# Latent attention over the context: the ends and beginnings of batches in other steps, and the residual norm in halves

## The reference, cut to the stage that is touched

```python
# layer 2, cross attention: x is the context (4, 77, 128), latents the stream (4, 512, 128), H = 8 heads of DH = 64
xn = _ln(x, g_x, b_x)
ln = _ln(latents, g_l, b_l)
q = ln @ w_q
kv_in = jnp.concatenate([xn, ln], axis=1)
k, v = jnp.split(kv_in @ w_kv, 2, axis=-1)
q, k, v = (split(q) * scale, split(k), split(v))
sim = jnp.einsum('bhid,bhjd->bhij', q, k)
sim = jnp.where(m, sim, -jnp.finfo(sim.dtype).max)
attn = jax.nn.softmax(sim, axis=-1)
out = jnp.einsum('bhij,bhjd->bhid', attn, v)
return _ln(out @ w_out, g_o, b_o)
# and around it, in the decoder
x = _layernorm(x + _L2_xattn_ref(ctx_1024, x, ...), axis=-1)
```

## Times and profile before

| | us |
|---|---|
| median of three executions | 2083.51 |
| lowest, highest | 2081.59, 2091.36 |
| the profiled execution | 2109.39 |
| its span | 2107.5 |
| the stage's loop in it, 1069.96 to about 1398 | some 328 |

### The profile page before, as it was taken

The page is one execution under the profiler, slowest core; times in us unless marked ns, Lnnn a source line. Parts: engine busy times, 40 slices in busy tenths (PEclk is TensorE's granted clock), DMA queues, the critical chain, the costliest instruction groups (busy, mean ns, idle before and its releaser), DMA issues. The chain is left out here.

```text
span 2107.5 us, 33370 instructions
## 1 busy us (share of the span) xinstructions
PE 1716.1 (81%) x11732; PEld 1022.0 (48%) x11822; DVE 1422.6 (68%) x3275; ACT 1075.5 (51%) x2294; POOL 416.6 (20%) x576
## 2 busy tenths in 40 slices
PE   4779858999977999985789999973699988796773
PEld 3546533333365666663644444432345444464662
DVE  4546578888764776765666767767699999575224
ACT  3346526777723445444455565543477777463221
POOL 0110030000032666652200000001200000100654
PEclk8999889999978999997999999995699999997896
DMA  4000000000025888861000000000000000001454
GB/s 121 1 1 2 1 1 0 1 1 1 1 94 199 315 327 324 334 238 42 1 1 0 1 1 1 1 1 18 1 1 2 2 1 1 1 2 51 136 156 129
DMA packets 42862, 132.29 MB, mean 63 GB/s; under 512 B 7106, under 2 KB 22635, under 8 KB 37611
## 3 DMA queue, kind: packets, MB, share of 16 engines
q1 hardware_dynamic: 32523, 116.98, 15.9%
q0 software_dynamic: 4992, 10.23, 1.5%
q10 hardware_dynamic: 5184, 2.95, 0.5%
HBM read 120.27 MB, written 14.58 MB: 64 GB/s over the span
## 5 line engine op out<-in xcount | busy, mean ns | idle before, releaser
L160 POOL TENSOR_SCALAR rstd<-MV 128x2 f32<-128x2 f32 (+1 forms) x100 | 27.0, 270 | 1014.6 <-DVE MV L128 1008.9
L855 DVE TENSOR_REDUCE l1aM<-PS 128x2 f32<-128x1024 f32 x128 | 152.9, 1220 | 22.6 <-PE PS L611 20.5
L773 ACT ACTIVATE l1aE<-PS 128x512 f32<-128x512 f32 x256 | 140.8, 595 | 48.7 <-PE PS L640 45.4
L773 ACT ACTIVATE l3aE<-PS 128x512 f32<-128x512 f32 (+3 forms) x256 | 102.5, 442 | 47.6 <-PE PS L644 44.8
L855 DVE TENSOR_REDUCE l3aM<-PS 128x2 f32<-128x256 f32 (+3 forms) x128 | 101.3, 819 | 20.7 <-PE PS L613 19.6
L2748 ACT COPY PT<-PS 128x512 f32<-128x512 f32 x128 | 68.9, 590 | 87.7 <-PE PS L2659 87.4
L2838 DVE TENSOR_REDUCE M<-PS 128x1 f32<-128x589 f32 x128 | 92.4, 764 | 24.0 <-PE PS L2648 23.7
L1879 PE MATMUL PS<-WB,H 128*128 128x512 f32 x234 | 107.7, 597 | 0.0
L2754 ACT ACTIVATE E<-PS,M 128x589 f32<-128x589 f32 x128 | 95.9, 763 | 19.4 <-DVE M L2838 19.3
L883 DVE SCALAR_TENSOR_TENSOR l3aE<-l3aE,l3aLB 128x2048 f32<-128x2048 f32 (+1 forms) x64 | 94.9, 1483 | 2.7 <-ACT l3aE L773 2.7
L611 PE MATMUL PS<-l1aKS,l1aQS 128*128 128x512 bf16 x249 | 76.8, 388 | 16.2 <-DVE l1aQS L878 5.5
(11 more groups left out here) (686 smaller groups left out, 4488.2 us busy)
## 6 DMA issues: line engine op xcount, KB each, us to landing
WB<-in_experts SPq DMA_DIRECT2D x39, 1286.0 KB
TB<-mixed_tails SPq DMA_DIRECT2D x39, 768.5 KB
WB<-in_experts SPq DMA_DIRECT2D x39, 384.0 KB
mixed_tails<-in_tails SPq DMA_DIRECT2D x1, 2305.5 KB, 12.2
cols_fold_sb<-in_cols_fold SPq DMA_DIRECT2D x1, 1676.0 KB, 12.1
mixed_tails<-in_tails SPq DMA_DIRECT2D x1, 1537.0 KB, 16.1
mixed_tails<-WB SPq DMA_DIRECT2D x2, 768.5 KB, 4.2
cols_l2x_sb<-in_cols_l2x SPq DMA_DIRECT2D x1, 1154.0 KB, 9.1
```

Source lines behind the costliest of these rows:

```text
L773: nc.scalar.activation(E[0:kn, home(m, kt) + j, q0:S], PS[0:kn, 4 + n % 2, q0:S], ACT.Exp, scale=SCALE).then_inc(exp_done, 1)
L855: v.tensor_reduce(M[:, m % 2, qt, 2 * hp:2 * hp + 2], PS[:, bank:bank + 2, 0:kc], AX, ALU.max, negate=True).then_inc(pair_free, 1)
```

## The change

The table of endings gets eight entries instead of six: I and Y are split into halves of two of the four row tiles each (I0, I1, Y0, Y1). The steps within the batch become these:

| unit | before | after |
|---|---|---|
| L, M, T, U | 6, 7, 8, 9, late | 0, 2, 3, 4, late |
| W, X, G, H | 5, 6, 7, 8 | 5, 6, 7, 8 |
| I | 9 | 10 and 12 (halves) |
| Y | 10 | 14 and 15 (halves) |
| the 14 projection units, two to a step | 9 to 15 | 8 to 14 |

```diff
+    ENDING = ("W", "X", "G", "H", "I0", "I1", "Y0", "Y1")
...
-            for i, c in enumerate("WXGHIY"):
-                late.setdefault(s0 + 5 + i, []).append((c, b - 1))
+            for c, at in zip(ENDING, (5, 6, 7, 8, 10, 12, 14, 15)):
+                late.setdefault(s0 + at, []).append((c, b - 1))
...
-            for i, u in enumerate(todo[:4]):
-                late.setdefault(s0 + 6 + i, []).append(u)
+            for u, at in zip(todo[:4], (0, 2, 3, 4)):
+                late.setdefault(s0 + at, []).append(u)
             for i, u in enumerate(todo[4:]):
-                (late, early)[i % 2].setdefault(s0 + 9 + i // 2, []).append(u)
+                (late, early)[i % 2].setdefault(s0 + 8 + i // 2, []).append(u)
...
-                elif kind == "I":
+                elif kind == "I1":
                     k.norm_gpsimd(pool, b, b)
...
-                elif kind == "I":
+                elif kind in ("I0", "I1"):
                     dve.wait_ge(y_done, 3 * b + 3)
-                    k.norm_stats(dve, Y[:, :, :], step, b)
-                elif kind == "Y":
-                    k.norm_apply(dve, normed, b, b)
+                    half = int(kind[1])
+                    k.norm_half_stats(Y[:, HALVES[half]], step, b, HALVES[half])
+                elif kind in ("Y0", "Y1"):
+                    k.norm_half_apply(dve, normed, b, b, int(kind[1]))
```

More of the change, by code:

```diff
@@ L2518, in latent_attention @@
         if b:
-            for i, c in enumerate("WXGHIY"):
-                late.setdefault(s0 + 5 + i, []).append((c, b - 1))
+            for c, at in zip(ENDING, (5, 6, 7, 8, 10, 12, 14, 15)):
+                late.setdefault(s0 + at, []).append((c, b - 1))
         if b + 1 < BT:
             todo = head(b + 1)
-            for i, u in enumerate(todo[:4]):
-                late.setdefault(s0 + 6 + i, []).append(u)
+            for u, at in zip(todo[:4], (0, 2, 3, 4)):
+                late.setdefault(s0 + at, []).append(u)
             for i, u in enumerate(todo[4:]):
-                (late, early)[i % 2].setdefault(s0 + 9 + i // 2, []).append(u)
-    for i, c in enumerate("WXGHIY"):
+                (late, early)[i % 2].setdefault(s0 + 8 + i // 2, []).append(u)
+    for c in ENDING:
         late.setdefault(NG + 1, []).append((c, BT - 1))
@@ L2820, in misc @@
                     ins.then_inc(y_done, 1)
-                elif kind in "GH":
+                elif kind in ("G", "H"):
                     dve.wait_ge(y_done, 3 * b + 1 + (kind == "H"))
```

## The result

Fifteen executions of each kernel, in alternation on one chip: 2089.47 us median before (2081.24 to 2099.23), 2076.72 us after (2073.96 to 2084.15). The ratio is 0.9947, its 95% interval 0.9934 to 0.9959, so the change takes away 0.53%, or 11.1 us (8.6 to 13.8; the two medians by themselves lie 12.8 apart, which is inside that). In a later series, where the kernel before takes 2114.36 us, it was 0.9954 (0.9937 to 0.9971). The forecast of 0.54% is met in size, and the time lies in the range, 4.4 us above 2072.3, as the kernel before also ran 6.0 us longer here than the 2083.51 that the forecast started from. But the sum behind it was wrong in one of its four batches, and in what it took for the clock of the kernel before; these two errors hid each other, and that is luck.

A forecast was written before the change was run, and what follows sets the result against it. PE was taken as the bound, with only its waits to win. Batches 0 to 3 gave -2.9, -4.0, -3.5 and -0.9, sum -11.3, taken as 11.2 us: 2083.5 becomes 2072.3, range 2068 to 2078.

The forecast's parts named there:

- What bounds the kernel: Batches 1 and 2: PE, working 82.03 of 88.23 us; only its 6.2 us of waits can be won.
- The price of a piece of DVE work: Plain steps: a maximum delayed by d makes the step max(P, 3.62 + d); beside two units, up to some 1.8 us free.
- The wait in step 13: Step 13: PE's V unit waits for the copy of C's bank behind I1, 0.9 us (0 to 1.62).
- Batches 1, 2, 3: Sums of step changes in these batches: -4.0, -3.5 and -0.9 us.
- Batch 0, "-2.9": Batch 0: L and M cost +1.45 and +1.27, outweighed by savings in steps 7, 9 and 15; sum -2.9 us.
- rival 4: Steps 1 to 4 of batch 0: longer PE idle time drops the clock to 1.2 GHz; 2085 or more, chance 0.02.
- The loop stands at clock 1.00 in every batch: Whole loop: full clock in every batch, so the 11.2 us gain carries over to the median of 2083.5.
- 1 (dearer waits): Bank 7's handovers, the copy behind I1 or ACT's latents copy cost more; 2075, gain 8 to 9, chance 0.19.
- 2 (DVE is the bound): Steps 8 to 14: H, I0, I1, Y0 cost in full, work only moved; 2079 to 2083, chance 0.07.
- 3 (wider covers): No stall at step 13, L's delay hidden in step 1; 2069, gain 13 to 14, chance 0.13.

The follow-up runs named there:

- the beginnings alone: Against the kernel before: L, M, T, U and the projections placed as changed, I at 9 and Y at 10 whole; ratio 0.9926 (0.9901 to 0.9952), loop 319.3 us.
- PE kept at work: The changed kernel with four unused matmuls added in PE's waits in steps 1 and 2 of batch 0; ratio to before 0.9931 (0.9911 to 0.9950).

## Why the size came out right, and which step of the prediction failed

**What bounds the kernel.** Right. PE's work in batches 1 and 2 is 81.6 us after the change (82.03 before), the waits fell from 6.1 to 2.7 us in batch 1, and the batch went with them, 3.99 us.

**The price of a piece of DVE work.** Right within 0.2 us wherever it was used: steps 1, 3, 7, 9 of batch 1 at 5.01, 4.92, 4.86, 6.47 for 4.96, 4.89, 4.86, 6.46; U cost 0.1 in step 4, not 0.24. What lies beside two units was even cheaper than allowed: up to 1.8 us was called free, 2.28 us cost nothing in the run with the beginnings alone.

**The wait in step 13.** Right in place and cause, as the run with I1 one step earlier shows; its size was 1.05, not 0.9. The half of I that the change put ahead of C's copy is why the beginnings alone have a loop as short as the whole change.

**Batches 1, 2, 3.** Right: -4.0, -3.4, -0.8 for -4.0, -3.5, -0.9.

**Batch 0, "-2.9": the step that failed.** It was +0.6 against the profile that it was made from, and 1.9 less than the mean of the four profiles with the old beginning (81.2, 83.4, 85.2, 85.1). The ledger of L, M, and of steps 7, 8, 9 and 15 was right (78.3 us with PE kept at work, 78.4 forecast), but the clock fell twice, at a price of 3.5 us (step 2 at 5.76 for 3.72, step 4 at 5.10 for 3.72). The sum had put this at nothing. The step that failed is the argument against rival 4: that an idle time of 2.4 us stood in step 7 at clock 1.00, so one of 2.3 us in step 1 would be harmless too. That clock was read from one execution. In other executions of the same kernel it falls behind that very wait, where step 9 hides the price; in batch 0 no later step takes it back. Rival 4 itself had the place right and the cause only in part: the fall in step 2 set in before L had made the wait longer, and came without L, while the fall in step 4 is only seen where M stands ahead of it.

**"The loop stands at clock 1.00 in every batch" (the sum).** Wrong as a statement on the kernel before: it was one execution. In nine of the ten profiles without filling matmuls the clock fell in batch 0; only the first is free of it. This error hid the other: the loop of before is 328.1, 330.2 and 332.7 us in its three profiles, mean 330.3, and that of the changed kernel 320.4 twice. So the difference is 9.9 us on the average of the profiles, between 7.7 and 12.3, and the ratios give 11.1 (8.6 to 13.8) and, in the later series, 9.7. The forecast of 11.2 came out because the clock's fall costs both kernels much the same, which it had no reason to count on. Whether the change makes it surer or dearer (four times 3.5 us, against 0, 2.1, 3.9 and 3.9 with the old beginning) these few profiles don't settle.

**Rivals.** 1 (dearer waits): no wait on ACT in steps 4 and 9 appeared. 2 (DVE is the bound): no; steps with two units stayed at 5.56 to 5.68 beside H and I0, and PE's waits, not DVE's work, went with the time. By the rule of the Trainium skill (Perfetto Trace Analysis, Identifying the Most-Contended Engine) DVE would be the engine to relieve. The runs speak against that in this stage: with DVE at 62.99 us before and 62.27 after in batch 1, taking 3.4 us of PE's waits away made it 3.99 us shorter. 3 (wider covers): no. 4 (the clock): the fall was there, its price 3.5 us and not over 11. The chance of 0.02 was for a slower kernel, which did not come; that the clock would fall at all had been given no chance and no term of its own. A gain clear of 0.5% was given 0.56 and one below 0.42; the measured 0.53% sits on that line.

## What to carry to other kernels

Where two engines take turns at nearly the same length, price a moved piece by the step that it lands in: here M, 1.3 us, cost 1.08 in a step with no other work for TensorE, and even 2.28 us cost nothing beside two projection units. Before moving a piece, look at what stands behind it in its own queue: 1.1 us of norm ahead of one bank's copy cost as much as the piece itself. And read the granted clock in more than one execution before taking it for a property of the kernel, above all where it is the argument for putting a term of the sum at nothing.

## What was not expected of the hardware

The granted clock of TensorE fell to about half, its level of 1.2 GHz, in batch 0's step 2 (0.50 to 0.58 over the step) around waits of 1.60 and 0.86 to 0.90 us in the kernel before, in two of three executions of identical instructions, and of 1.60 and 2.32 us in the changed one. Two matmuls of unused work (1.02 to 1.13 us each when alone), set into these waits, held it at 1.00 in all three runs that had them (four in the first), and made the batch 3.5 to 3.9 us shorter in two of them against the same order without. The waits ahead were the same where it fell and where it did not, so they alone don't decide it. What differs in the trace is the clock before the loop, 0.98 over 12 us against 0.92 to 0.96; whether that decides was not tried. The same shows in small in batch 3's step 11: 5.4 us instead of 4.75 behind a wait of 1.7 us, in three of the five profiles in which I stands whole there, and in step 8 of batches 1 and 2, behind 2.38 us, in five places of ten.
